# An attention and feed-forward kernel on one core: ScalarE copies the transposed probabilities before the exponentials in all three of its slots

## What is computed

```python
scores = einsum('bhsr,btr->bhst', q_lat, c_kv) + einsum('bhsd,btd->bhst', q_rope, k_rope)
scores = where(causal, scores / sqrt(DN + DR), min)
probs = softmax(scores, axis=-1)
out_lat = einsum('bhst,btr->bhsr', probs, c_kv)
out = einsum('bhsr,hdr->bhsd', out_lat, wuv)
x = x + out.reshape(b, s, H * DV) @ w_out
```

## Time and profile before

| | us |
|---|---|
| median of 3 runs (1224.57 to 1225.35) | 1225.11 |
| the profiled execution, own time | 1225.95 |
| its span, first to last instruction | 1224.1 |
| PE busy | 1129.4 |
| DVE busy | 936.0 |
| POOL busy | 741.1 |
| ACT busy | 597.5 |

### The profile page before, as it was taken

The page is one execution under the profiler, slowest core; times in us unless marked ns, Lnnn a source line. Parts: engine busy times, 40 slices in busy tenths (PEclk is TensorE's granted clock), DMA queues, the critical chain, the costliest instruction groups (busy, mean ns, idle before and its releaser), DMA issues.

```text
span 1224.1 us, 24129 instructions
## 1 busy us (share of the span) xinstructions
PE 1129.4 (92%) x7312; PEld 933.0 (76%) x7312; DVE 936.0 (76%) x3049; ACT 597.5 (49%) x1698; POOL 741.1 (61%) x943
## 2 busy tenths in 40 slices
PE   5988999999797999999988799999989699999996
PEld 4746788888696788888777678888869578888876
DVE  5767887887676888888667688788767688878855
ACT  3644556555123655555413455555612365555541
POOL 1407887777213987777412788777721398877741
PEclk9998999999898999999989899999989899999998
DMA  9750000000100000000100000000010000000000
GB/s 258 209 160 1 2 1 2 2 1 1 35 36 2 1 1 2 2 1 1 36 26 10 2 2 1 1 1 1 1 35 36 2 2 1 2 1 1 1 1 35
DMA packets 21674, 28.00 MB, mean 23 GB/s; under 512 B 10247, under 2 KB 12039, under 8 KB 20907
## 3 DMA queue, kind: packets, MB, share of 16 engines
q1 hardware_dynamic: 19178, 21.71, 5.8%
q10 hardware_dynamic: 2368, 4.72, 1.2%
HBM read 22.23 MB, written 4.19 MB: 22 GB/s over the span
## 4 chain that ended last, share of the span: by engine, by line
PE 78%; DVE 7%; POOL 6%; issue 5%; ACT 2%; DMA 1%; SPq 1%; POOLq 0%; DVEq 0%; ACTq 0%
PE Y L911 14%; PE Y L885 11%; PE XZ L870 11%; PE Y L834 11%; PE XZ L851 6%; PE XZ L850 6%; PE XZ L849 5%; PE Y L616 5%; PE XZ L616 4%; POOL prob L576 2%; POOL q_sums L496 2%; PE XZ L595 2%; POOL qT_lo L501 2%; DVE q_turned L1440 1%; DVE stats L1151 1%
## 5 line engine op out<-in xcount | busy, mean ns | idle before, releaser
L1124 ACT ACTIVATE prob<-XZ,small 128x512 f32<-128x512 f32 (+3 forms) x512 | 266.6, 526 | 290.6 <-DVE small L1493 289.2
L576 POOL TENSOR_TENSOR prob<-prob,small 128x512 f32<-128x512 f32 (+3 forms) x512 | 361.2, 723 | 57.2 <-DVE small L1448 40.7
L1493 DVE CUSTOM_DVE_ANT_0 XZ<-XZ,mask 128x512 f32<-128x512 f32 (+3 forms) x512 | 245.0, 510 | 114.5 <-issue 112.2
L496 POOL TENSOR_TENSOR q_sums<-q_sums,q_turned 64x512 f32<-64x512 f32 (+2 forms) x136 | 165.2, 1215 | 160.3 <-DVE q_turned L1441 156.6
L870 PE MATMUL XZ<-ident,prob 128*128 128x128 f32 x1280 | 196.9, 276 | 5.0 <-POOL prob L576 4.5
L849 PE MATMUL XZ<-kT_hi,qT_hi 128*128 128x512 f32 (+3 forms) x512 | 179.0, 350 | 17.3 <-POOL qT_lo L501 11.8
L501 POOL TENSOR_TENSOR qT_lo<-q_sums,qT_hi 128x512 fp32r<-128x512 f32 (+2 forms) x136 | 166.3, 1223 | 40.5 <-ACT qT_hi L1091 39.8
L870 PEld LDWEIGHTS XZ<-ident,prob 128*128 128x128 f32 x1280 | 150.0, 140 | 45.4 <-issue 15.7
L850 PE MATMUL XZ<-kT_lo,qT_hi 128*128 128x512 f32 (+3 forms) x512 | 166.8, 326 | 0.0
L851 PE MATMUL XZ<-kT_hi,qT_lo 128*128 128x512 f32 (+3 forms) x512 | 166.3, 325 | 0.0
L885 PE MATMUL Y<-probT,ckv 128*64 128x384 f32 (+2 forms) x1280 | 152.3, 383 | 3.2 <-issue 0.9
(11 more groups left out here) (199 smaller groups left out, 2296.1 us busy)
## 6 DMA issues: line engine op xcount, KB each, us to landing
wout_nat<-in_L_attn_w_out_dram SPq DMA_DIRECT2D x16, 512.0 KB, 5.1
out_dram<-x_sb SPq DMA_DIRECT2D x16, 256.0 KB, 2.0
x_next<-_attn_hidden_states_dram SPq DMA_DIRECT2D x12, 256.0 KB, 3.7
wbase_nat<-in_L_ffn_W_base_dram ACTq DMA_DIRECT2D x1, 1024.0 KB, 5.4
x_sb<-_attn_hidden_states_dram ACTq DMA_DIRECT2D x4, 256.0 KB, 6.8
nope_a<-_L_attn_w_q_up_nope_dram ACTq DMA_DIRECT2D x1, 1024.0 KB, 6.8
rope_a<-_L_attn_w_q_up_rope_dram SPq DMA_DIRECT2D x1, 1024.0 KB, 8.8
rope_bb<-_L_attn_w_q_up_rope_dram SPq DMA_DIRECT2D x2, 512.0 KB, 11.4
```

The costliest lines, as they stand in the source:

```text
L496: nc.gpsimd.tensor_tensor(q, q, turned, ALU.add).then_inc(q_sum_set, 1)
L576: last = nc.gpsimd.tensor_tensor(prob[u % RING][:, c:c + w], prob[u % RING][:, c:c + w], inv_sum[:, u % RING, m:m + 1].broadcast_to([P, w] ...
L1124: last = nc.scalar.activation(prob[u % RING][:, c:c + w], score_ps[u % 2][:, c:c + w], ACT.Exp, bias=neg_max[:, u % RING, m:m + 1], scale= ...
L1493: last = nc.vector.tensor_tensor_reduce(bank, bank, mask[:, S - w:S], -1.0, HIGHEST, ALU.add, ALU.min, neg_max[:, u % RING, m:m + 1])
```

## The change

ACT's copy of a transposed unit stood ahead of the slot's exponentials in the slot k = 2 and behind them in the slots k = 0 and 3. Now it stands ahead of them in all three. Nothing is added or taken away; no other engine's stream changes.

```diff
@@ -1112,7 +1112,7 @@
                         v = u - T_LAG
                         copies = known(g, u, T_LAG) and within(g, u, SLOTS - 1 + T_LAG) and v % UNITS in ACT_BANKS
-                        if copies and k == 2:
+                        if copies:
                             copy_probT(act, nc.scalar, b, g, v)
                         if within(g, u, SLOTS - 1):
                             n = 80 * b + BODY * g + u
@@ -1125,8 +1125,6 @@
                                                             ACT.Exp, bias=neg_max[:, u % RING, m:m + 1], scale=-1.0,
                                                             accum_out=row_sum[:, u % RING, m:m + 1])
                             last.then_inc(prob_set, 1)
-                        if copies and k != 2:
-                            copy_probT(act, nc.scalar, b, g, v)
                     attention(work, TAIL)
```

## The result

| | before | after |
|---|---|---|
| median of 5 runs, us | 1225.11 (1224.57 to 1225.41) | 1230.24 (1230.01 to 1231.04) |
| profiled execution, us | 1225.95 | 1230.01 |
| its span, us | 1224.1 | 1228.2 |

What follows compares the result with a forecast made beforehand. TensorE, busy for 92% of the span, was taken as the bound; 0.78 - 0.36 + 0.76 + 0.2 = 1.38 us a sample, 5.5 us in four, gave 1230.6 us, range 1226.5 to 1238.

Steps and rivals of the forecast that it cites:

- The direct stalls: Slot k = 3, pairs 1 and 2: TensorE's scores wait for unit 3's late exponentials, 0.78 and 0.76 us a sample.
- the steady pairs cost nothing: From pair 3 on, slot k = 4's output matmuls cover the later exponentials; room of 0.71 us, no cost.
- the slot k = 0: Copy of unit 2 ahead of unit 0's exponentials: 1.96 us against a tightest distance of 1.95; 0 to 0.2, taken as 0.
- What is given back: Between the two stalls, TensorE's waits of 0.18 for POOL and 0.18 for ScalarE go: -0.36 us, range -0.36 to 0.
- the first place: First of the two direct stalls, in pair 1, counted at 0.78 us a sample.
- Behind pair 2 nothing is given back: After the second stall, of 0.76 us, no wait is won back, since TensorE has no gaps left.
- The end: Last pair: unit 3's exponentials delay VectorE's reciprocal, then scaling and transposes; 0.2 us a sample, between 0 and 0.22.
- room 0.7: Steady pairs: POOL's scaling, behind the query copy 0.9 later, is done at 467.13, wanted at 467.83; no cost.
- No change: Rival: room is enough everywhere, ScalarE being idle half the time; 1224 to 1226.6 us, likeliest 1225.1; chance 0.14.
- Steady pairs losing: Rival: exponentials or POOL's chain overrun the room in every pair; 0.2 each gives 9.6 us more, 1240; chance 0.08.
- The clock: Rival: TensorE's granted clock falls at the new stalls, 6.9 us more, 1237.5; chance 0.06.

Runs made afterwards that it cites:

- e3: Kernel before, with the copy also ahead of the exponentials in slot k = 3 of pairs 3 to 13 only; 1224.98 us, ratio 0.9999.
- e8: Kernel before, with the second output of a pair moved from slot k = 4 to k = 2 in all pairs; 1228.66 us against 1224.63.
- e9: Changed kernel, with the second output of a pair moved from slot k = 4 to k = 2; 1274.78 us against 1224.63 for the kernel before.
- e2: Kernel before, with the copy ahead of the exponentials in slots k = 0 and 2, behind in k = 3; 1225.30 us, ratio 0.9995.
- e1: Kernel before, with the copy ahead of the exponentials in slots k = 2 and 3, behind in k = 0; 1230.19 us against 1225.27.
- e12: Kernel before, with the second output in slot k = 2 for pairs 3 to 13 and in k = 4 for 14 and 15; 1221.72 us against 1225.34.
- e5: Kernel before, with the copy also ahead in slot k = 3 of pairs 14 and 15 only; 1227.29 us against 1225.14.
- e6: Kernel before, with ScalarE waiting for the transposes ahead of the exponentials in slot k = 3, copy still behind; 1230.53 us against 1225.14.
- e11: As e6, with the second query head's copy moved from slot k = 4 to ahead of the unit's copy in k = 3; 1227.12 us against 1225.34.
- e7: Kernel before, with the copy behind the exponentials in slot k = 2 as well, so in all three; 1275.85 us, ratio 1.0424.
- e10: Changed kernel, with the second query head's copy moved from slot k = 4 to k = 3, between unit's copy and exponentials; 1247.43 us, ratio 1.0174.

## Why the prediction was right, and where its terms were off

- **The direct stalls** were counted at 0.78 and 0.76. The changed kernel shows 2.33 - 1.55 = 0.78 and 2.34 - 1.57 = 0.77: right. So is that the steady pairs cost nothing (e3), that the output covers them (e8, e9), and that the slot k = 0 adds nothing to the time (e2).
- **What is given back** between the two: 0.36 was taken, which leaves 0.42 at the first place; the ruler has 0.36. The size is right by luck. The 0.18 listed in the earlier trace rows is idle time behind a modelled end, and the waits are longer when they are read from start to start. Before, the transposes at 415.28 start 1.15 us after their slot's scores, in the changed kernel 0.80 (416.67 - 415.87); the scores at 418.55 start 0.78 after their transposes, in the changed kernel 0.36 (419.94 - 419.58). So 0.35 + 0.42 = 0.77 was there to be given back, and all of it is, as much as the direct stall:

```profile
414.13 0.50 PE L849 MATMUL XZ<-kT_hi,qT_hi 128*128 128x512 f32 x1
...
417.77 0.60 PE L870 MATMUL XZ<-ident,prob 128*128 128x128 f32 x4
```

- **What is lost at the first place all the same** are two things of nearly equal size, neither of them in the sum with a size. One is the slot k = 0. Its distance of 1.95 contained the wait for POOL that is given back; without it the scores at 417.47 start 0.80 after the transposes at 416.67, 0.39 later than the 0.41 of the earlier trace rows (415.69 - 415.28). The prediction had put this between 0 and 0.2 and took 0. The other is the third path, over the output latents' copy and VectorE. In e1, where the slot k = 0 is as before, the same scores start 0.41 after their transposes, and yet pv 1 is as late: TensorE then waits at the scores of unit 3, which start 0.73 after theirs, and there the third path ends. In the changed kernel TensorE comes there as late by itself (the exponentials are over at 419.84, its scores start at 419.94). That e2 costs nothing and e1 everything is true of the sum; it doesn't show that the slot k = 0 loses nothing.
- **"Behind pair 2 nothing is given back"** was wrong: the ruler has 0.58 and not 0.76 at the second place. In the second sample's pair 3, slot k = 1, the transposes started 1.02 after their slot's scores before (426.91 - 425.89) and 0.81 after (428.85 - 428.04): a wait was there to be given back. The list of waits on which the step rested begins at 437.6, after this place. The size, 0.18 a sample, is 0.7 us in all. That "no gaps left" was too strong is seen in the table of stretches too: TensorE is busy for 99.33 of 100 us in the kernel before and for 100.00 in e12.
- **The end** was counted at 0.2 a sample and is 0.48 (e5: 0.33 and 0.16). The 0.16 is the delay of the reciprocal that was priced at 0.2. The missed 0.33 is the step "room 0.7" for POOL's scaling of unit 3: it was worked out for a steady pair and used for all, but the last pair has no query matmuls, so TensorE wants the scaled unit over a microsecond earlier. The rule was right and one of its places was not looked up.
- The two misses, 0.7 us too much and 1.1 too little in four samples, nearly cancel in the sum; the forecast, 1230.6, is nearer to 1230.24 than its terms deserve. That is luck, as is the size at the first place.
- **What the sum did not see** is that behind the direct stalls stand others of the same size: the path over the query copy and POOL at pair 2 (e6, e11), which the prediction named and for which it found room only in the steady pairs, and the one over the output latents' copy and VectorE at pair 1, whose first operation it named as late and did not follow. They hardly change the sum, but they decide what a repair would bring.
- **The rivals.** No change: excluded by the interval. Steady pairs losing: e3 excludes it beyond some 0.02 us a pair (its interval ends at 1.0008, 1 us in 44 pairs). The clock: the mean granted clock of the profiled executions is 0.970 before and 0.972 after, and in the changed kernel it is 1.00 from 405 to 433 us, over the new stalls. It did fall behind the longer stalls of e7 and e10. The rule weighed there, of the Trainium skill's "Perfetto Trace Analysis", section "Identifying the Most-Contended Engine", finds the right engine, TensorE. That an engine at 49% could then be reordered freely doesn't follow, and here cost 5.1 us.

## What to carry to other kernels

An in-order engine that is half idle has no free order: putting an operation that waits ahead of one that is ready makes everything behind it late by the wait. Which of two operations goes first is read from the distance to their readers, in the slots where the bounding engine has the least work between (e7 and the change are the same rule in opposite slots). A room that is worked out in the steady state has to be worked out again for the first and the last turns, since there the work that covers it is missing, and for every reader behind the moved operation, also one that hangs on it over another engine. The bounding engine's waits are best read from start to start and compared with the same place elsewhere, since an idle time behind a modelled end shows only a part of them.

## What the runs showed that was not expected

pv can start earlier behind ScalarE's copy of unit 4 in the last sample, which stands outside of the loop over the samples, than inside of the loop. The kernel before, in the second sample, ScalarE's copy and TensorE's pv:

```profile
458.67 0.60 ACT L367 ACTIVATE probT<-XZ 128x512 f32<-128x512 f32 x1 [0.97 <-PE XZ L870]
```

```profile
459.50 2.38 PE L885 MATMUL Y<-probT,ckv 128*64 128x384 f32 x20
```

That is 0.23 us behind the copy's end. The last sample is read in e7, where pv waits for the copy there too:

```profile
1086.76 0.59 ACT L367 ACTIVATE probT<-XZ 128x512 f32<-128x512 f32 x1
```

```profile
1087.41 2.38 PE L885 MATMUL Y<-probT,ckv 128*64 128x384 f32 x20 [0.51 <-ACT probT L367]
```

Here it is 0.06 us, where e7 has 0.24 in the second sample (477.72 against the copy's end at 477.48). In the kernel before a pair takes 13.62 us in the loop and 13.49 outside of it. Moving an output ahead of pv took the difference away (e8 and e12 gain 0.12 a pair in the first three samples and nothing in the last). Why it is longer in the loop was not tried and stays open.
